# The last batch's first two contraction tiles of layer 2 as fp32r products of halves, and two of its output quarters finished by TensorE and ScalarE

## What is computed

```python
def reference(x, ...):
    x = x + L0(x)   # x @ W.T + (x @ A[label]) @ Bw.T * 0.5, rank 32
    x = x + L1(x)   # each element: one of 8 quantisation steps, by thresholds on |x|
    x = x + L2(x)   # x @ weight[adapter].T, 1024 x 1024
    x = x + L3(x)   # (x @ B[adapter].T) @ A[adapter].T, rank 16
    return x
```

## Time and profile before

| | |
|---|---|
| median of the runs | 460.23 us |
| the profiled execution | 459.77 us |
| its span | 458.0 us |
| TensorE busy | 446.3 us, 97% of the span |
| VectorE busy | 423.1 us, 92% |
| ScalarE busy | 357.5 us, 78% |
| GpSimd busy | 34.6 us, 8% |

### The profile page before, as it was taken

One profiled execution on the slowest core, in us unless ns is written; L12 is line 12 of the kernel. 1 busy time (PEld: TensorE's weight loads), 2 busy tenths in 40 slices (PEclk: granted clock), 3 DMA queues, 4 the chain that ended last, 5 costly groups with the idle time before them and its releaser, 6 DMA issues.

```text
span 458.0 us, 7875 instructions
## 1 busy us (share of the span) xinstructions
PE 446.3 (97%) x3118; PEld 408.1 (89%) x3118; DVE 423.1 (92%) x409; ACT 357.5 (78%) x330; POOL 34.6 (8%) x46
## 2 busy tenths in 40 slices
PE   7999999999999999999999999999999998999995
PEld 6899999889898999989998999989998998998784
DVE  4889999999899998999899998999969999999983
ACT  5699999987799777977799775997569958676730
POOL 1000011010101000000101000110100101000000
PEclk9999999999999999999999999999999999999999
DMA  7963453596359835687459835486353626378022
GB/s 287 334 241 105 92 135 100 134 224 212 82 167 244 248 89 151 184 220 228 82 180 232 244 92 149 143 215 174 76 188 117 168 63 166 122 212 318 1 92 92
DMA packets 35352, 75.62 MB, mean 165 GB/s; under 512 B 3956, under 2 KB 14068, under 8 KB 34548
## 3 DMA queue, kind: packets, MB, share of 16 engines
q1 hardware_dynamic: 30420, 61.50, 40.3%
q0 software_dynamic: 4896, 13.63, 16.8%
HBM read 53.10 MB, written 8.39 MB: 134 GB/s over the span
## 4 chain that ended last, share of the span: by engine, by line
PE 64%; DVE 23%; issue 8%; DMA 2%; ACT 2%; SPq 1%; DVEq 0%; ACTq 0%
PE l_ps L925 31%; PE l_ps L990 18%; DVE quant L784 8%; DVE cand L758 6%; PE l_ps L1002 5%; PE l_ps L1018 3%; DVE cand L766 2%; DVE x L736 2%; PE bx_ps L951 2%; PE bx_ps L1037 2%; DVE quant L778 1%; DMA a_raw<-a 1%; PE l_ps L935 1%; DVE x L835 1%; DMA adapter_ids<-adapters 1%
## 5 line engine op out<-in xcount | busy, mean ns | idle before, releaser
L990 PE MATMUL l_ps<-x,w_sb 128*128 128x256 f32 x672 | 150.3, 380 | 0.9 <-DVE x L736 0.9
L784 DVE COPY_PREDICATED quant<-mask,cand 128x2048 f32<-128x2048 int8 (+2 forms) x77 | 146.0, 1897 | 0.4
L990 PEld LDWEIGHTS l_ps<-x,w_sb 128*128 128x128 f32 x672 | 125.9, 190 | 19.4 <-issue 2.1
L566 ACT ACTIVATE cand<-x,inv_delta 128x2048 f32<-128x2048 f32 (+2 forms) x88 | 134.4, 1527 | 8.8 <-DVE quant L778 7.0
L576 ACT ACTIVATE mask<-magnitude,thr_bias 128x2048 fp8e5<-128x2048 f32 (+2 forms) x77 | 117.5, 1526 | 9.0 <-DVE quant L784 8.2
L758 DVE TENSOR_SCALAR cand<-cand,delta 128x2048 f32<-128x2048 f32 (+2 forms) x88 | 87.6, 996 | 7.7 <-ACT cand L566 7.4
L766 DVE TENSOR_SCALAR cand<-cand,lower,upper 128x2048 f32<-128x2048 f32 (+2 forms) x88 | 92.8, 1055 | 0.4
L925 PE MATMUL l_ps<-x_hi,w_hi 128*128 128x256 f32 x512 | 86.1, 290 | 1.9 <-ACT w_hi L467 1.0
L925 PE MATMUL l_ps<-x_hi,w_lo 128*128 128x256 f32 x512 | 82.8, 283 | 0.0
L925 PE MATMUL l_ps<-x_lo,w_hi 128*128 128x256 f32 x512 | 82.5, 283 | 0.0
L925 PEld LDWEIGHTS l_ps<-x_hi,w_hi 128*128 128x128 f32 x512 | 71.0, 191 | 7.7 <-issue 4.1
(11 more groups left out here) (84 smaller groups left out, 384.6 us busy)
## 6 DMA issues: line engine op xcount, KB each, us to landing
w_sb<-w SPq DMA_DIRECT2D x60, 384.0 KB, 3.8
out<-x SPq DMA_DIRECT2D x32, 256.0 KB, 2.3
x_raw<-x SPq DMA_DIRECT2D x15, 512.0 KB, 5.9
w_edge<-w SPq DMA_DIRECT2D x28, 256.0 KB, 3.5
w_lo<-w_edge POOLq DMA_DIRECT2D x28, 256.0 KB, 4.7
x_lo<-x_raw POOLq DMA_DIRECT2D x6, 1024.0 KB, 8.6
cand<-w SPq DMA_DIRECT2D x7, 512.0 KB, 7.6
x<-a SPq DMA_DIRECT2D x7, 512.0 KB, 3.4
```

Source lines behind the costliest of these rows:

```text
L566: act.activation(cand[:, c % CANDS, 0:n], x2_unit(u), ACT.Identity, bias=ROUND, scale=inv_delta[:, k:k + 1]).then_inc(rounded, 1)
L784: dve.copy_predicated(y, mask[:, m % MASKS, 0:n].bitcast(I8), t).then_inc(merged, 1)
L990: last = nc.tensor.matmul(l2_bank(b, q)[:, i * S:(i + 1) * S], w2_block(b, o, k), x2[:, b % SLOTS, k * S:(k + 1) * S], start=(i == 0 and k ...
```

## The change

The two first contraction tiles of the last batch's layer 2 become products of halves. A new function `last_first_part` stands in place of `last_layer2(0)`: it makes tiles 2 and 3 plain for all eight outputs, then waits for the halves of the activations and makes tiles 0 and 1 as three fp32r matmuls each. The halves of the weights go into free parts of `x_hi` and `x_lo`; ScalarE makes them in pairs for outputs 0 to 3, in steps 1 and 4 of unit 8, and one by one for outputs 4 to 7, in steps 1 to 4 of unit 9. GpSimd adds the raw weights, the two pairs ahead of `add_edges(6, 3)`. VectorE splits the activations after unit 8. At the end quarter 2 is treated as quarter 3 was: TensorE puts x3 into PSUM by products with the identity (`add_up`), and ScalarE copies the result out. The order of the loads in SyncE's queue is the same as before; `load_last_edge` only raises another semaphore.

```diff
+ADDED_UP = (3, 2)
@@ SyncE
                 sp.dma_start(edge_tile(B - 1, o), w2[...])\
-                  .then_inc(last_w2_loaded[o], 16)
+                  .then_inc(last_edge_loaded[o], 16)
@@ GpSimd
+            def add_last_pair(q):
+                pool.wait_ge(w2_neg_done, 4 * SPLIT + q)
+                pool.dma_start(last_edges(x_lo, 2 * q, 2), x_raw[...], accum_op=ALU.add)\
+                    .then_inc(w2_added[q], 16)
+            def add_last_edge(o):
+                pool.wait_ge(w2_neg_done, 4 * SPLIT + 3 + o - RING)
+                pool.dma_start(last_edges(x_lo, o, 1), edge_tile(B - 1, o), accum_op=ALU.add)...
             for s in range(1, B):
                 ...
+                if s == SPLIT:
+                    for q in range(2):
+                        add_last_pair(q)
                 add_edges(s - 1, 3)
                 ...
+            for o in range(RING, T):
+                add_last_edge(o)
@@ ScalarE
+            def split_last_pair(q):
+                for o in (2 * q, 2 * q + 1):
+                    act.wait_ge(last_edge_loaded[o], 16)
+                act.wait_ge(l0_done, 2 * (B - 1))
+                hi = last_edges(x_hi, 2 * q, 2)
+                act.activation(hi, x_raw[:, 2 * q * EW:2 * (q + 1) * EW], ACT.Copy).then_inc(w2_hi_done, 1)
+                act.wait_ge(w2_hi_done, 4 * SPLIT + q)
+                act.activation(last_edges(x_lo, 2 * q, 2), hi.bitcast(F32), ACT.Copy, scale=-1.0)...
+            def split_last_edge(o):
+                act.wait_ge(last_edge_loaded[o], 16)
+                ... (the same two activations on one tile)
                 elif u == LAST:
+                    if j == 1:
+                        split_last_pair(0)
                     if j == 2:
                         split_a3(s - 1)
                     if j == 3:
                         drain_l0(s, 1)
+                    if j == 4:
+                        split_last_pair(1)
                     if j == 5:
                         split_edges(s - 1, 3)
+                elif u == LAST + 1:
+                    if j in (1, 2, 3, 4):
+                        split_last_edge(RING + j - 1)
@@
-            act.wait_ge(l3_done, 4 * (B - 1) + LAST_ORDER.index(3) + 1)
-            act.activation(x3[:, 3 * CW:4 * CW], l3_bank(B - 1, 3), ACT.Copy).then_inc(last_out_done, 1)
+            for q in ADDED_UP:
+                act.wait_ge(l3_done, 4 * (B - 1) + LAST_ORDER.index(q) + 1)
+                act.activation(x3[:, q * CW:(q + 1) * CW], l3_bank(B - 1, q), ACT.Copy).then_inc(last_out_done, 1)
@@ VectorE
-                if UNITS[u][0] < SPLIT and u > 0:
+                if 0 < u <= LAST:
                     split_x2(UNITS[u][0])
...
-                if q != 3:
+                if q not in ADDED_UP:
                     finish(b, q)
@@ TensorE
+            def last_first_part():
+                b = B - 1
+                pe.wait_ge(x0_done, 2 * B)
+                pe.wait_ge(x2_done, LAST + 1)
+                for o in range(T):
+                    pe.wait_ge(last_w2_loaded[o], 16)
+                    for k in range(EDGE, PARTS[1]):
+                        nc.tensor.matmul(...plain..., start=(o % 2 == 0 and k == EDGE), stop=False)
+                pe.wait_ge(x2_split_done, B)
+                x2h, x2l = x2_halves(b)
+                for o in range(T):
+                    if o >= RING:
+                        pe.wait_ge(last_edge_added[o - RING], 16)
+                    elif o % 2 == 0:
+                        pe.wait_ge(w2_added[o // 2], 16 * B)
+                    hi, lo = last_edges(x_hi, o, 1), last_edges(x_lo, o, 1)
+                    for w, v in ((hi, x2h), (hi, x2l), (lo, x2h)):
+                        for k in range(EDGE):
+                            nc.tensor.matmul(...fp32r..., start=False, stop=False)
-            last_layer2(0)
+            last_first_part()
             ...
             for q in range(4):
                 low_rank3(B - 1, q)
-
-            for i in range(2):
-                nc.tensor.matmul(l3_bank(B - 1, 3)..., ident[:, :], x3[...], start=(i == 0), stop=False)
+                if q in ADDED_UP and q < 3:
+                    add_up(q)
+            add_up(3)
```

More of the change, by code:

```diff
@@ L128, in build @@
         last_w2_loaded = [sem(f"last_w2_loaded{o}") for o in range(T)]
+        last_edge_loaded = [sem(f"last_edge_loaded{o}") for o in range(T)]
+        last_edge_added = [sem(f"last_edge_added{o}") for o in range(RING, T)]
         w2_used = sem("w2_used")
@@ L238, in split_pair, with last_edges, x2_halves @@
             return tiles[:, first:first + 2, :]
+        def last_edges(halves, first, n):
+            return halves[:, 0, first * EW:(first + n) * EW]
+        def x2_halves(b):
+            if b == B - 1:
+                return x_hi[:, b % 2, 0:EX], x_lo[:, b % 2, 0:EX]
+            return x2_hi[:, :], x2_lo[:, :]
         def a3_raw(b):
@@ L245, in b3_tile, with edge_count @@
             return m[:, k * w:(k + 1) * w]
+        def edge_count(b, q):
+            return 4 * b + q + (3 if (b, q) == (SPLIT - 1, 3) else 1)
         fold = parts[:, 0:QUAD]
@@ L343, in store @@
                     sp.wait_ge(out_done, b * 4 + q + 1)
-                elif q == 3:
-                    sp.wait_ge(last_out_done, 1)
+                elif q in ADDED_UP:
+                    sp.wait_ge(last_out_done, ADDED_UP.index(q) + 1)
                 else:
-                    sp.wait_ge(out_done, b * 4 + q + 1)
+                    sp.wait_ge(out_done, b * 4 + [p for p in LAST_ORDER if p not in ADDED_UP].index(q) + 1)
                 sp.dma_start(out[b, q], x3[:, q * CW:(q + 1) * CW]).then_inc(out_stored[q], 16)
@@ L1005, in layer2 @@
                     last.then_inc(l2_done, 1)
+            def last_first_part():
[5 more added lines that the diff above has]
+                    for k in range(EDGE, PARTS[1]):
+                        nc.tensor.matmul(l2_bank(b, o // 2)[:, o % 2 * S:(o % 2 + 1) * S], w2_block(b, o, k),
+                                         x2[:, b % SLOTS, k * S:(k + 1) * S], start=(o % 2 == 0 and k == EDGE),
+                                         stop=False)
+                pe.wait_ge(x2_split_done, B)
[8 more added lines that the diff above has]
+                        for k in range(EDGE):
+                            nc.tensor.matmul(l2_bank(b, o // 2)[:, o % 2 * S:(o % 2 + 1) * S],
+                                             w[:, k * P:(k + 1) * P], v[:, k * S:(k + 1) * S],
+                                             start=False, stop=False)
             def last_layer2(part, quarters=range(4)):
                 b = B - 1
-                if part == 0:
-                    pe.wait_ge(x0_done, 2 * B)
                 pe.wait_ge(x2_done, LAST + part + 1)
@@ L1020, in last_layer2 @@
                                                     x2[:, b % SLOTS, k * S:(k + 1) * S],
-                                                    start=(i == 0 and k == 0), stop=(i == 1 and k == T - 1))
+                                                    start=False, stop=(i == 1 and k == T - 1))
                     if part == len(PARTS) - 2:
@@ L1050, in layer3 @@
                     pe.wait_ge(a3_split_done, b + 1)
-                on_x3 = b == B - 1 and q == 3
+                on_x3 = q in ADDED_UP
                 for i in range(2):
@@ L1056, in layer3, with add_up @@
                 last.then_inc(l3_done, 1)
+            def add_up(q):
+                for i in range(2):
+                    nc.tensor.matmul(l3_bank(B - 1, q)[:, i * S:(i + 1) * S], ident[:, :],
+                                     x3[:, (2 * q + i) * S:(2 * q + i + 1) * S], start=(i == 0), stop=False)
             def layer3_pair(b, q):
@@ L1108, in _ @@
                 low_rank3(B - 1, q)
-            for i in range(2):
-                nc.tensor.matmul(l3_bank(B - 1, 3)[:, i * S:(i + 1) * S], ident[:, :],
-                                 x3[:, (T - 2 + i) * S:(T - 1 + i) * S], start=(i == 0), stop=False)
+                if q in ADDED_UP and q < 3:
+                    add_up(q)
+            add_up(3)
             for q in LAST_ORDER:
```

34 lines of the change are left out of this document (22 added, 12 removed).

## The result

The changed kernel takes 480.97 us (median of 4 runs, 480.61 to 481.05) against 460.02 us for the kernel before; the ratio is 1.0454 (95% interval 1.0439 to 1.0468). The profiled execution took 481.03 us for a span of 479.1 us. Forecast were 478.9 us, between 477.5 and 482.5, and a rival at 480.6 us in which the matmuls behind the second gap are slow. The time fell near that rival, and the trace shows its mechanism.

What follows compares the result with a forecast made beforehand. The end was taken as set by when ScalarE, paced by VectorE, reaches drain_bx in step 5 of unit 10, with TensorE waiting. 16.6 + 1.2 + 0.9 = 18.7 us more gave 478.9 us, range 477.5 to 482.5.

Steps and rivals of the forecast that it cites:

- the second gap: TensorE's wait for ScalarE at sum_bx of batch 6, forecast at 5.6 us.
- The stop of ScalarE: Unit 8, step 1: ScalarE waits 21.3 us for edge loads, making VectorE's step 3 16.6 us late; chance 0.66, 478.9 us.
- the landing: Edge loads of batch 7 arrive in x_raw at 408.5 us, 3.8 us after issue (bounds 408.3 and 409.6).
- Nothing is caught up: VectorE sets the pace in the rest of unit 8, so the 16.6 us reach ScalarE's drain_bx whole.
- The split of x2: VectorE's split_x2 behind unit 8, in front of unit 9, adds 1.2 us to VectorE's chain.
- The quarter put up: add_up(2), two plain matmuls between the last batch's low-rank products of quarters 2 and 3, adds 0.87 us before layer 3.
- the stores would give nothing back: At the end, stores leave SyncE one by one, 0.45 us each: no gain taken, bounds 0 and 0.45 us.
- The clock: Rival: matmuls from sum_bx of batch 6 on start at half speed, losing 1.7 us (480.6) or twice that (482.3); chance 0.27.
- the main case: ScalarE's wait for the edge loads in unit 8 sets the time, without slow matmuls behind sum_bx: 478.9 us, chance 0.66.
- the first gap: TensorE idles 14.4 us at quarter 2 of batch 6's layer 2, waiting for VectorE's drain_l2.
- the 3.4 us of half speed: Assumed slow stretch of TensorE from sum_bx of batch 6 on, as long as perhaps at the kernel's start; 1.7 us lost.
- The faster rival: The products' saving of 1.2 us reaches the end, decided at sum_bx of batch 6: 458.6 us, chance 0.02.

Runs made afterwards that it cites:

- the wait alone: Kernel before, plus only ScalarE's wait in step 1 of unit 8 for the loads of edges 0 and 1 of the last batch: 474.69 us, ratio 1.0315.
- the experiment alone: Kernel before, with only quarter 2 of x3 also put into PSUM by TensorE and copied out by ScalarE: 461.26 us, ratio 1.0026.
- the loads a little early: Changed kernel with the last batch's four edge loads moved just ahead of the four weight loads of batch 6: 469.43 us.
- The split on ScalarE and a DMA: Changed kernel, edge loads early, only quarter 3 put up, x2 split by ScalarE and a GpSimd-issued DMA instead of VectorE: 460.13 us, ratio 1.0013.

## Why the prediction held, and where it was off

*The stop of ScalarE* was read from three rows of the kernel before, the place in ScalarE's order, the issue of the loads and VectorE's want of candidate 3, and it is what happened: forecast 16.6 us, measured 15.8 us, and 14.6 us for the wait alone. The term was 0.8 us too large in the landing: the earlier trace rows gave 3.7 to 4.1 us, and the loads of the changed kernel land sooner (median 3.1 us). That median comes with four issues in 2.03 us that no GpSimd DMA meets. The forecast had moved the issues for that, and kept the landing.

*Nothing is caught up.* The claim that VectorE sets the pace of unit 8 behind the stop held: 15.8 us late at step 3, 15.7 us at the unit's end.

*The split of x2* was put at 1.2 us and costs 1.6. The wait for VectorE's own result ahead of it is 0.46 us, where the sum had 0.1; in unit 7, from which the row came, four other instructions of the kernel before lie between the unit's end at 382.96 us and the split:

```profile
385.16 1.91 DVE L741 TENSOR_TENSOR x<-l_ps,x 128x512 f32<-128x512 f32 x3
386.96 0.71 DVE L741 TENSOR_TENSOR x<-bx_ps,x 128x512 f32<-128x512 f32 x1
```

*The quarter put up* was put at 0.9 us and costs 1.2 (the experiment alone: 1.2 by the ratio). The sum took the price of two plain products in a row; here they break a row of low-rank products in two, and both changes cost. The trace of the kernel before had the better price, since the two products that put up quarter 3 stand in it, 1.07 us from row to row:

```profile
451.05 1.13 PE L1111 MATMUL l_ps<-x,ident 128*128 128x256 f32 x4
452.12 1.22 PE L1054 MATMUL l_ps<-bx_split,a_split 128*128 128x256 f32 x8
```

That the stores would give nothing back held: from layer 3 to the end it is 5.9 us in both kernels.

*The clock* was the rival with chance 0.27, at 480.6 us, and it is the one that came; the main case, with 0.66, had put this term at nothing. Its mechanism and its place were as written there: slow behind the first gap without harm (13.46 us, then 7.09 in place of 5.34 us, which shortened the second gap), slow behind the second on the path. Forecast were 1.7 us or twice that, measured 3.0 us, and 1.6 us with the loads a little early. No row shows the 3.4 us of half speed from which the forecast's loss was taken: by the earlier trace rows the matmuls are fast at 4.75 us, and the first of the trace starts at 1.53. The reason given against it, that the second gap would be short, was half right: 4.06 us in place of 5.6. It was enough all the same. The Trainium skill (TensorE: Matmul & The Clock Gate, Part 1) had the rule, an idle engine falls back to half its clock, and the traces here agree: 0.50 behind 13.46, 5.34 and 4.06 us, 1.00 behind 0.81 us. In the profiled executions with waits of 3.19 and 3.27 us the clock stayed at 1.00. The rule deserved more than a quarter of the chance.

That the time came within 0.4 us of this rival's 480.6 is in part luck. The two terms that were too small (0.4 + 0.3 us) and the one that was too large (0.8 us) nearly cancel, and this execution was 0.56 us ahead from its start. With the 3.0 us of the clock that makes 21.1 us in the pair of traces where the forecast had 18.7, 2.4 us more. The median lies 2.1 us above the forecast, since the forecast had put the median 0.46 us above the profiled execution, as in the kernel before, and here the two agree within 0.1 us.

*The faster rival* failed at the place named for it: the saving of 1.2 us was real (from the first row of part 0 to `low_rank3` it is 445.36 - 432.62 = 12.7 us, before 432.22 - 418.24 = 14.0) and turned to waiting at `sum_bx`. The split on ScalarE and a DMA shows the same: with 48 products of halves and little other cost the time is that of the kernel before.

## What to carry to other kernels

Before a step is put into an in-order queue, find the issue of the data that it waits for in the other queue's timeline: an operand that used to be wanted 30 us later may be loaded only just in time for that, and one wait without work can cost almost fifteen microseconds. Work saved on an engine that waits for another later on the same path comes back as a longer wait, and on TensorE a longer wait can cost more than was saved, since it then starts again slowly; the step it waits for has to move first. When a load becomes late or a pass gets faster, look also at the order in which it consumes what is loaded.

## What the hardware showed that was not expected

- The length of TensorE's slow stretch doesn't follow that of the wait ahead of it: 0.50 for 6 us behind a wait of 4.06 us, and 1.00 again after some 4 us behind 13.46 us in the same execution.
- With a wait of 3.2 us on TensorE executions of one kernel took 462.6 to 467.0 us, and 462.4 to 463.0 us once the wait was filled with useless products (four executions each; the slow matmuls themselves were not seen).
- Useless matmuls can pay: nine of them, 3.9 us on an engine that waits, give back 3.0 us in the rows behind.
- Two GpSimd instructions of together 2.0 us cost VectorE 1.2 us in `tensor_scalar` instructions beside them (1.48 us in place of 0.47).
- A change of TensorE between low-rank products with 64-column weights and full products costs some 0.1 to 0.2 us (1.06 in place of 0.87 us, 0.58 in place of 0.44 to 0.47 us), and one from plain to fp32r products at full width 0.18 us (0.42 in place of 0.24).
- In two of the profiled executions a single store took 1.47 and 1.78 us to be issued, with a median of 0.35 us; such scatter doesn't come from TensorE.
